# A recommendation tower on one core: low pieces that signal one by one, and two groups of transposes at other places in TensorE's order

## The reference

```python
e = jnp.stack([tbl_0[ids[:, 0]], ..., tbl_26[ids[:, 26]]], axis=1)   # (512, 27, 128)
dot = jnp.einsum('bnd,bmd->bnm', e, e)
z = flat[:, idx]                       # the 351 pairs i < j of flat = dot.reshape(512, 27 * 27)
h = jnp.concatenate([z, dense_ctx], axis=1)          # (512, 367)
h = jnp.maximum(h @ W_top1 + b_top1, 0.0)            # W_top1 (367, 512)
h = jnp.maximum(h @ W_top2 + b_top2, 0.0)            # W_top2 (512, 256)
y = h @ W_top3                                       # (512, 1)
```

## Time and profile before

| | us |
|---|---|
| median of 3 runs | 106.79 (106.44 to 106.99) |
| the profiled execution | 106.66 |
| its span in the trace | 104.8 |
| TensorE busy in it | 99.6 |
| DVE, ScalarE, GpSimd busy | 79.5, 71.5, 62.1 |

### The profile page before, as it was taken

The page is one execution under the profiler, slowest core; times in us unless marked ns, Lnnn a source line. Parts: engine busy times, 40 slices in busy tenths (PEclk is TensorE's granted clock), DMA queues, the critical chain, the costliest instruction groups (busy, mean ns, idle before and its releaser), DMA issues.

```text
span 104.8 us, 2680 instructions
## 1 busy us (share of the span) xinstructions
PE 99.6 (95%) x1012; PEld 86.4 (82%) x1012; DVE 79.5 (76%) x240; ACT 71.5 (68%) x151; POOL 62.1 (59%) x68
## 2 busy tenths in 40 slices
PE   5989997999999999999999998999999988999992
PEld 5858785888888888888887797999999978999980
DVE  5599999999999899998969949996259540952212
ACT  4486999599896999969796359893358431961240
POOL 3777777777887777777777777777777300000000
DMA  2887998978849767589922222322222200000000
GB/s 54 237 195 221 195 222 177 229 184 189 199 102 245 176 167 170 117 236 327 353 74 53 55 58 53 85 68 59 73 53 59 68 6 0 6 12 12 6 1 0
DMA packets 5541, 12.57 MB, mean 120 GB/s; under 512 B 2066, under 2 KB 2804, under 8 KB 5401
## 3 DMA queue, kind: packets, MB, share of 16 engines
q1 hardware_dynamic: 3585, 8.44, 30.2%
q0 software_dynamic: 1920, 3.94, 16.0%
q10 hardware_dynamic: 24, 0.02, 0.1%
HBM read 12.15 MB, written 0.00 MB: 116 GB/s over the span
## 4 chain that ended last, share of the span: by engine, by line
PE 77%; DVE 7%; DMA 5%; ACT 4%; issue 2%; SPq 2%; DVEq 0%
PE acc L408 19%; PE acc L400 17%; PE gram_ps L438 12%; PE acc L456 11%; PE tr_ps L372 6%; PE acc L476 5%; DMA table<-in_tbl 5%; PE gram_ps L456 3%; DVE onehot L579 3%; DVE pairs L532 2%; PE gram_ps L381 2%; PE tr_ps L476 2%; DVE lo L585 2%; ACT embT L636 1%; SPq L295 1%
## 5 line engine op out<-in xcount | busy, mean ns | idle before, releaser
L358 POOL DMA_INDIRECT emb<-in_tbl,ids_sb x60 | 61.3, 1021 | 19.4 <-issue 18.0
L579 DVE TENSOR_SCALAR onehot<-idrel 125x512 fp32r<-125x512 f32 x90 | 32.1, 425 | 1.8 <-ACT idrel L650 1.8
L400 PE MATMUL acc<-onehot,hi 125*128 125x512 f32 x102 | 26.3, 400 | 0.2 <-DVE onehot L579 0.2
L408 PE MATMUL acc<-onehot,lo 125*128 125x512 f32 x102 | 25.7, 393 | 0.8 <-DVE lo L585 0.8
L408 PEld LDWEIGHTS acc<-onehot,lo 125*128 125x128 f32 x102 | 18.8, 188 | 5.9 <-DVE lo L585 2.1
L400 PEld LDWEIGHTS acc<-onehot,hi 125*128 125x128 f32 x102 | 18.6, 188 | 4.1 <-issue 0.3
L532 DVE COPY pairs<-gram_ps 26x96 f32<-26x96 f32 (+1 forms) x64 | 16.5, 258 | 7.1 <-PE gram_ps L438 5.8
L532 ACT COPY pairs<-gram_ps 26x96 f32<-26x96 f32 (+1 forms) x64 | 15.2, 238 | 7.5 <-PE gram_ps L438 6.1
L585 DVE TENSOR_TENSOR lo<-table,hi 125x256 fp32r<-125x256 f32 x51 | 18.1, 412 | 0.0
L636 ACT COPY embT<-acc 128x512 f32<-128x512 f32 (+2 forms) x13 | 13.4, 1048 | 6.8 <-PE acc L408 6.7
L438 PEld LDWEIGHTS gram_ps<-embT 128*58 128x58 f32 x512 | 14.2, 133 | 2.3 <-issue 1.8
(11 more groups left out here) (48 smaller groups left out, 56.2 us busy)
## 6 DMA issues: line engine op xcount, KB each, us to landing
table<-in_tbl SPq DMA_DIRECT2D x8, 480.0 KB
table<-in_tbl SPq DMA_DIRECT2D x3, 600.0 KB
w_sb<-in_W SPq DMA_DIRECT2D x1, 1024.0 KB, 8.2
emb<-in_tbl,ids_sb POOLq DMA_INDIRECT x60
w_sb<-in_W SPq DMA_DIRECT2D x1, 512.0 KB, 9.4
table<-in_tbl SPq DMA_DIRECT2D x2, 240.0 KB
pairs<-pairs SPq DMA_DIRECT2D x16, 15.0 KB
table<-in_tbl SPq DMA_DIRECT2D x8, 20.0 KB
```

Source lines behind the costliest of these rows:

```text
L358: pool.indirect_dma_start(emb[:, t % EMB_RING, gathered_features.index(f), :], None, tables[f], bass.IndirectOffsetOnAxis(ids_sb[:, t, f:f ...
L400: return nc.tensor.matmul(acc[:, b, 0:batch], hi[0:ROWS_K, b, c, :], one_hot(k, c), start=(c == 0), stop=False)
L408: return nc.tensor.matmul(acc[:, b, 0:batch], lo[0:ROWS_K, b, c, :], one_hot(k, c), start=False, stop=(c == CHS[k] - 1))
L579: nc.vector.tensor_scalar(one_hot(k, one), idrel[0:ROWS_K, b, 0:batch], float(one), None, ALU.is_equal).then_inc(onehot_by_dve, 1)
```

## The change

There are two edits.

First, each low piece (two chunks, one instruction of DVE) signals `lo_ready` by itself, 51 signals in place of 14. TensorE waits before every second low product for the piece that it needs, and SyncE's wait counts pieces (`pieces_to`) to the same point as before.

```diff
         def parts_to(k):
 
             return k + min(k, EARLY)
+
+        def pieces_to(k):
+
+            return sum(CHS[:k]) // 2
...
-                    sp.wait_ge(lo_ready, parts_to(k - RING + 1))
+                    sp.wait_ge(lo_ready, pieces_to(k - RING + 1))
...
-                    for n, part in enumerate(parts(k)):
-                        if c == part.start:
-                            pe.wait_ge(lo_ready, parts_to(k) + n + 1)
+                    if c % 2 == 0:
+
+                        pe.wait_ge(lo_ready, pieces_to(k) + c // 2 + 1)
...
-                        last = nc.vector.tensor_tensor(lo[0:ROWS_K, b, two, :], table[0:ROWS_K, r, two, :],
-                                                       hi[0:ROWS_K, b, two, :], ALU.subtract)
-                    last.then_inc(lo_ready, 1)
+                        nc.vector.tensor_tensor(lo[0:ROWS_K, b, two, :], table[0:ROWS_K, r, two, :],
+                                                hi[0:ROWS_K, b, two, :], ALU.subtract).then_inc(lo_ready, 1)
```

Second, the list. The third tile's first group of transposes goes ahead of the first gram, its second and third group move up by a place each, and the fourth tile's last group goes ahead of `h2` of the second tile:

```diff
-        STEPS = tr(1, [3]) + [("gram", 0, 0), ("gram", 0, 1)] + tr(2, [0]) + [("gram", 1, 0)] + tr(2, [1]) + [("gram", 1, 1)]
+        STEPS = tr(1, [3]) + tr(2, [0]) + [("gram", 0, 0), ("gram", 0, 1)] + tr(2, [1]) + [("gram", 1, 0)] + tr(2, [2])
...
-        STEPS += [("h1", 1, None)] + tr(3, [1, 2]) + [("h2", 1, None)] + tr(3, [3])
+        STEPS += [("gram", 2, 1), ("h1", 1, None)] + tr(3, [1, 2, 3]) + [("h2", 1, None)]
```

More of the change, by code:

```diff
@@ L228, in tr @@
             return [("transposes", t, g) for g in groups if (t, g) in ORDER[len(AT_LOOKUP):]]
-        STEPS = tr(1, [3]) + [("gram", 0, 0), ("gram", 0, 1)] + tr(2, [0]) + [("gram", 1, 0)] + tr(2, [1]) + [("gram", 1, 1)]
-        STEPS += tr(2, [2]) + [("h1", 0, None)] + tr(2, [3]) + [("h2", 0, None), ("gram", 2, 0)] + tr(3, [0]) + [("gram", 2, 1)]
-        STEPS += [("h1", 1, None)] + tr(3, [1, 2]) + [("h2", 1, None)] + tr(3, [3])
+        STEPS = tr(1, [3]) + tr(2, [0]) + [("gram", 0, 0), ("gram", 0, 1)] + tr(2, [1]) + [("gram", 1, 0)] + tr(2, [2])
+        STEPS += [("gram", 1, 1), ("h1", 0, None)] + tr(2, [3]) + [("h2", 0, None), ("gram", 2, 0)] + tr(3, [0])
+        STEPS += [("gram", 2, 1), ("h1", 1, None)] + tr(3, [1, 2, 3]) + [("h2", 1, None)]
         t = TILES - 1
```

## The result

The changed kernel takes 106.02 us (median of 20 runs) against 106.60 us for the kernel before, measured again beside it in 20 runs. The ratio is **0.9927, with a 95% interval of 0.9906 to 0.9948**: 0.7% faster, 0.5 to 0.9%. The forecast was 106.15 us, 0.6 us under the runs of before. One of the 20 executions took 117.17 us and has no part in the ratio. The profiled execution after took 106.09 us, with a span of 104.3 us (before 106.66 and 104.8).

The account below looks back on a forecast made before the run. TensorE, busy 95%, bounds the kernel; pieces free 1.4 us, but moved transposes then wait for GpSimd's gather at 83.95, so the last gram begins at 86.30, not 86.90: gain 0.60 us, 106.15 us, range 105.2 to 106.9 with two rivals included.

Parts of the forecast that it names:

- Pieces: TensorE's look-ups: waiting per low piece, not per low half, returns 1.07 us in look-up 2, 0.26 in the last; 1.4 taken.
- The cost of 37 waits: TensorE's low products: the added waits cost 1 to 3 ns each, 0.1 us in all at most.
- The third tile's transposes: Moved ahead of the first gram: gram 0.28 us later, h1 held by the moved rows; 0.2 us lost, hidden later.
- The gate: Last tile's last three transposes, moved ahead of h2, wait for GpSimd's last gather, seen at 83.95 us; TensorE idles 1.3 us.
- The last gram: On TensorE behind h2: begins at 86.30 us in place of 86.90, the tail of 17.9 us unchanged; gain 0.60 us.
- In words: Whole change: pieces give 1.4 us; the new place of three transposes gives most of it back to GpSimd's clock.
- (a): Last three transposes: the gather is no gate, the bank's copy at 83.0 is; gain 1.45 us, 105.3 us; chance 0.13.
- (b): Look-ups: pieces bring nothing, the stall only moves to a later look-up; gain 0, 106.8 us; chance 0.14.
- (c): GpSimd: denser look-ups slow its gathers, making the kernel slower, 107.3 to 107.6 us; chance 0.05.
- (f): Last gather seen late, at 84.3 us, 0.8 us behind its last packets; gain 0.25 us, 106.5 us; chance 0.05.
- (d): TensorE's clock drops to the 1.2 GHz level after idling 1.3 us ahead of the gather; 108 us or more; chance 0.02.
- The other reading: GpSimd's gathers: look-ups ended 1.2 us sooner put one more gather in the fast part, worth 0.1 us.

Follow-up runs that it names:

- order only: The kernel before with the new list of steps, low halves signalled as before: 106.52 us against 106.62, ratio 0.9988.
- pieces only: The changed kernel with the old list of steps, so only the low pieces signal one by one: 105.50 us against the kernel before's 107.10, ratio 0.9854.
- the third tile's groups back: Changed kernel with the third tile's transposes at their old places, the last tile's last group still ahead of h2: 106.15 us against the kernel before's 107.01, ratio 0.9918.
- the extra gather: A 61st gather into an unread buffer ahead of the last group's three; ratios to the kernel before: 0.9985 in the kernel before, 1.0026 (107.27 us) in the changed kernel.
- the last group back: Changed kernel with the last tile's last transposes behind h2 again: 106.31 us against the kernel before's 106.62, ratio 0.9891.

## Why the prediction was right, step by step

- **Pieces.** Forecast 1.07 us back in look-up 2, 0.26 in the last, 1.4 in all (1.1 to 1.6). Measured 0.99, 0.25 and 1.45; 0.21 us came from the first look-ups (14.17 for 14.38), of which I had counted nothing. There, too, it was a wait for a low half: the first look-up's low products begin at 6.70 us for 7.04, and the wait of 0.17 us ahead of them is gone. How much of that is left by look-up 2 varies: in the other traces with pieces it begins between 14.17 and 14.55. Look-up 3 begins at 19.02, forecast near 19.0. DVE held: TensorE was 1.20 to 1.21 us early at look-ups 3, 4 and the last one's start.
- **The cost of 37 waits.** Forecast 0.1 us at most. The low half of a ten-chunk look-up takes 2.27 us in the chain of after as in that of before. Nothing is seen of them.
- **The third tile's transposes.** The first gram began 1.23 us early (forecast 1.4 - 0.28 = 1.12). `h1`'s second product does stand behind the moved rows, for 0.20 us, as forecast. The price of the whole was forecast at 0.2 us and measured at 0.20 (23.97 us for 23.77 from the look-ups' end to the eight transposes), and at 0.22 with the order only. It was hidden by the gate, as forecast, so no time shows it.
- **The gate.** Forecast at 83.95 us with 1.3 us of idle; measured 84.13 and 1.35. This is the term that was most off. The lag of the semaphore behind the last packets was taken from the moved rows as 0.4 us. Here the gather landed at 84.08, 2.67 us behind the start of its issue, with its last packets no later than 83.55: 0.5 us or a little more.
- **The last gram.** Forecast 86.30, measured 86.39, for 86.90 before. The gate was 0.18 us later than forecast and the way from it to the gram 0.09 us shorter (2.26 for 2.35), so half of the miss was made good by luck. The tail kept its length. The gain, forecast at 0.60 us, was 0.51 at the last gram, 0.57 between the profiled executions and 0.58 between the medians.
- **In words**, that the pieces give 1.4 us and the moved transposes give most of it back: shown, by pieces only (0.9854), order only (0.9988), the third tile's groups back (0.9918, so it is not they that take the gain), the row of 1.35 us and the extra gather in both kernels. That putting the last group alone back returns the gain is not shown (0.9891, between the two).
- **The rivals.** (a) fell with the idle ended by the gather, (b) with look-up 3 beginning 1.20 us early and with pieces only. (c) did not come: beside the look-ups the gathers keep their pace, and the last issue begins at 81.42 for 81.38. (f) is half true: 84.13 lies midway between its 84.3 and the forecast's 83.95, and the time nearer to the forecast. (d), the clock, stayed away in the profiled execution, but the clock did fall in two other profiled executions, as the last section shows.

What stands of the page "SBUF — State Buffer" of the Trainium skill, section "SBUF: two separate sides": by its rule, as the forecast read it, the end of the look-ups 1.2 us earlier should leave GpSimd's pace as it was, and the last issue moved by 0.04 us. The other reading, a gain of 0.1 us, is not seen in this pair, but one pair does not decide. One gather more did run fast (the one at 56.44 took 0.94 us, where the one at 56.32 took 1.03 before), and over all traces without a late GpSimd the last issue begins at 81.16 to 81.42 us with pieces and at 81.38 to 81.61 without, once the traces with a gather more or less are shifted by 1.25 us. That leans to the other reading, and executions differ by as much. The lock is not shown.

## What to carry to other kernels

A step can be moved ahead of idle time and still lose: what counts is whether what it waits for is tied to the engine that was sped up, or runs on a clock of its own, as a queue of gathers does. So ask of each moved step for the absolute time at which its last input lands, and keep it behind work that does not need that input; cover the copy behind it with some other ready piece (here a block of `h1`) instead of moving the step itself. And test two edits apart: here one was worth 1.5%, the other nothing, and both together half of the first.

## What the runs showed of the hardware

**A gather's issue can take far longer than its neighbours'.** In the profiled execution of pieces only, two gathers took 2.62 and 1.73 us where most of their neighbours take 1.03 to 1.09:

```profile
33.18 1.03 POOL L362 DMA_INDIRECT emb<-in_tbl,ids_sb  x1 [0.30 <-issue]
34.52 2.62 POOL L362 DMA_INDIRECT emb<-in_tbl,ids_sb  x1 [0.30 <-issue]
37.44 1.73 POOL L362 DMA_INDIRECT emb<-in_tbl,ids_sb  x1 [0.30 <-issue]
...
83.39 0.94 POOL L362 DMA_INDIRECT emb<-in_tbl,ids_sb  x1 [0.30 <-issue]
```

The last issue began 2 us late, and even in the old order the last three transposes waited for their gather:

```profile
85.97 0.55 PE L376 MATMUL tr_ps<-ident,emb 128*128 128x128 f32 x3 [0.91 <-DMA emb<-in_tbl,ids_sb]
```

The same pair, 2.62 and 1.73 us, stands in the changed kernel with the extra gather, at 48.02 us, and 2.62 followed by 10.13 us in one profile of the kernel with the last group back. No cause is shown. It means that the room ahead of a gather's use, about 1.6 us in the kernel before (use at 85.65, landing at 81.38 + 2.67) and none in the changed one, is also what an execution with such a stall lives on. Of executions over 110 us there are one in 20 of the changed kernel, one in 7 each of pieces only and the last group back, 3 in 13 of the changed kernel with the extra gather, and one in 93 of the kernel before. The two of them that were profiled, 114.64 and 110.83 us, both have such gathers; for the others it is not known.

**The clock can fall behind an idle, and the length of that idle alone does not say when.** In the profiled execution of the changed kernel with the extra gather, the late GpSimd and the extra gather came together and TensorE idled 3.91 us. Busy time by stretch (us, then busy PE, PEld, DVE, ACT, POOL, the granted clock, DMA share, GB/s):

```profile
86.00:87.00 1.00, 0.00 (x0) 0.00 (x0) 0.00 (x0) 0.00 (x0) 0.00 (x0) 1.00 0.30 66
87.00:88.00 1.00, 0.81 (x6) 0.81 (x7) 0.00 (x0) 0.23 (x1) 0.00 (x0) 0.80 0.00 0
...
90.00:91.00 1.00, 1.00 (x6) 0.86 (x5) 0.00 (x0) 0.00 (x0) 0.00 (x0) 0.50 0.00 0
91.00:92.00 1.00, 1.00 (x35) 0.92 (x36) 0.35 (x1) 0.00 (x0) 0.00 (x0) 0.99 0.00 0
```

The grant went from full to 0.50, the 1.2 GHz level, just when the work resumed, and back near 91 us; the same `h2` took 3.58 us in place of 1.95.

```profile
87.19 0.55 PE L384 MATMUL tr_ps<-ident,emb 128*128 128x128 f32 x3 [3.91 <-DMA emb<-in_tbl,ids_sb]
87.57 3.58 PE L488 MATMUL acc<-h1T,w_sb 128*128 128x128 f32 x16
```

That execution took 110.8 us. The profiled execution of the kernel with the last group back has both outcomes. Behind an idle of 3.14 us in the look-ups the clock stayed at 1.00; behind one of 2.18 us among the grams, with another of 1.06 us shortly before it, the grant was 0.50 from 73 to 75 us, and half a gram took 3.14 us in place of 1.92.

```profile
53.38 0.66 PE L376 MATMUL tr_ps<-ident,emb 128*128 128x128 f32 x4 [3.14 <-DMA emb<-in_tbl,ids_sb]
...
66.73 0.66 PE L376 MATMUL tr_ps<-ident,emb 128*128 128x128 f32 x4 [1.06 <-DMA emb<-in_tbl,ids_sb]
...
71.41 0.65 PE L376 MATMUL tr_ps<-ident,emb 128*128 128x128 f32 x4 [2.18 <-DMA emb<-in_tbl,ids_sb]
72.00 3.14 PE L442 MATMUL gram_ps<-embT 128*58 128x52 f32 x64
```

The idles of 1.35 us in the changed kernel and 1.08 us with the third tile's groups back left the clock at 1.00.
